# A 12-sublayer decoder on one core: router logits moved into the sublayer before, routing by packed one-hots on VectorE and ScalarE, gathers of the last combination started before all expert blocks are done

## The reference

```python
logits = x @ gate_weight.T                       # 1024 x 64
scores = softmax(logits)
topk_w, topk_idx = top_k(scores, 8)
topk_w = topk_w / sum(topk_w)
order = argsort(topk_idx.reshape(-1))            # 8192 pairs (token, expert), sorted by expert
g = ragged_dot(x_repeated[order], w_gate, sizes) # each expert: 256 -> 96
u = ragged_dot(x_repeated[order], w_up, sizes)
out = ragged_dot(silu(g) * u, w_down, sizes)     # 96 -> 256
y = sum(out_back_in_token_order * topk_w)        # 8 rows per token
x = layernorm(x + y)
```

## Time and profile before

| What | Before |
|---|---|
| Median of 3 runs | 1993.46 us (1992.19 to 1999.12) |
| The profiled execution's own time | 2002.99 us |
| Its span in the trace | 2001.2 us |
| PE, DVE, ACT, POOL busy | 76%, 60%, 41%, 29% of the span |
| Moved by DMA | 126.19 MB, 63 GB/s mean |
| HBM written | 18.74 MB |

### The profile page before, as it was taken

One profiled execution on the slowest core, in us unless ns is written; L12 is line 12 of the kernel. 1 busy time (PEld: TensorE's weight loads), 2 busy tenths in 40 slices (PEclk: granted clock), 3 DMA queues, 4 the chain that ended last, 5 costly groups with the idle time before them and its releaser, 6 DMA issues. The chain is left out here.

```text
span 2001.2 us, 26001 instructions
## 1 busy us (share of the span) xinstructions
PE 1519.1 (76%) x8419; PEld 924.1 (46%) x8419; DVE 1192.4 (60%) x2274; ACT 829.3 (41%) x1630; POOL 575.2 (29%) x585
## 2 busy tenths in 40 slices
PE   6899779985267477777899987998997945999900
PEld 4656435554143122245344444335564634888800
DVE  3537642246745799987999984543365464444343
ACT  3237421213624665634999972210463101333300
POOL 0100200212020699944000001112102426555375
PEclk9999889997689699998555558998798956999955
DMA  2100000011000000001343330000000005999932
GB/s 83 58 10 2 2 21 1 24 55 48 1 29 0 0 1 0 0 1 76 59 74 73 72 64 32 0 0 1 1 2 15 1 21 172 336 342 342 313 102 87
DMA packets 117813, 126.19 MB, mean 63 GB/s; under 512 B 75088, under 2 KB 93648, under 8 KB 116272
## 3 DMA queue, kind: packets, MB, share of 16 engines
q1 hardware_dynamic: 108512, 99.48, 16.3%
q0 software_dynamic: 9168, 25.05, 3.9%
HBM read 88.97 MB, written 18.74 MB: 54 GB/s over the span
## 5 line engine op out<-in xcount | busy, mean ns | idle before, releaser
L1639 POOL TENSOR_TENSOR l_drive<-l_area,l_xpad 128x512 f32<-128x512 f32 x128 | 158.4, 1270 | 88.6 <-ACT l_xpad L1657 88.6
L436 POOL TENSOR_TENSOR rstd<-var,minus_half 128x1 f32<-128x1 f32 x96 | 61.1, 637 | 368.2 <-DVE var L407 368.2
L1613 PE MATMUL psum<-l_drive,consts 128*128 128x512 f32 x256 | 136.2, 635 | 37.7 <-DVE l_drive L1704 37.7
L2032 ACT ACTIVATE l2x_rings<-psum,l2x_mx,l2x_q_s 128x1024 f32<-128x1024 f32 x128 | 154.3, 1205 | 8.6 <-DVE l2x_mx L2003 6.5
L1989 DVE TENSOR_REDUCE l2x_mx<-psum 128x1 f32<-128x1024 f32 x128 | 155.6, 1217 | 0.9 <-PE psum L1955 0.9
L1698 DVE TENSOR_TENSOR_SCAN l_state<-psum,l_drive 128x512 f32<-128x512 f32 x128 | 152.5, 1212 | 5.1 <-ACT psum L1670 4.5
L2510 POOL DMA_INDIRECT l3f_rows<-moe_rows,l3f_token_ids x127 | 120.6, 949 | 97.8 <-PE psum L2537 90.2
L1955 PE MATMUL psum<-l2x_kT,l2x_qT 48*128 48x512 bf16 x256 | 130.0, 612 | 14.1 <-ACT l2x_rings L2032 5.8
L355 ACT ACTIVATE XT<-psum 128x256 f32<-128x256 f32 x88 | 33.9, 385 | 242.5 <-PE psum L376 242.5
L2548 PE MATMUL psum<-l3f_xT,l3f_of_expert 128*96 128x128 f32 x1016 | 134.0, 276 | 0.0
L2595 DVE COPY l3f_xT<-psum 128x256 f32<-128x256 f32 x127 | 53.9, 424 | 133.0 <-PE psum L2537 123.4
(11 more groups left out here) (477 smaller groups left out, 3340.2 us busy)
## 6 DMA issues: line engine op xcount, KB each, us to landing
l3f_of_expert<-in_experts SPq DMA_DIRECT2D x127, 320.0 KB
moe_out<-l3f_y_out SPq DMA_DIRECT2D x127, 128.0 KB
arena<-in_pack SPq DMA_DIRECT2D x1, 3660.0 KB, 12.1
arena<-in_pack SPq DMA_DIRECT2D x1, 3277.0 KB, 10.7
arena<-in_pack SPq DMA_DIRECT2D x1, 2688.0 KB, 9.8
arena<-in_pack SPq DMA_DIRECT2D x1, 2303.0 KB, 8.7
l3f_rows<-moe_rows,l3f_token_ids POOLq DMA_INDIRECT x127
arena<-in_pack SPq DMA_DIRECT2D x1, 1538.0 KB, 6.7
```

The source lines that it names most:

```text
L1613: nc.tensor.matmul(sum_bank(c), k.identity[:, :], drive[:, (4 * i + c) % 8, :], start=n == 0, stop=n == states - 1, skip_group_check=True) ...
L1639: nc.gpsimd.tensor_tensor(drive[:, (4 * i + c) % 8, :], dx[:, c, half * HALF:(half + 1) * HALF], b_copy[:, i % 2, :], ALU.mult).then_inc(d ...
L2032: nc.scalar.activation(e[:, i % 3, :], score_banks(i).rearrange("p b t -> p (b t)"), ACT.Exp, bias=mx[:, i % 4, 1:2], scale=q_s[:, i:i + 1 ...
```

## The change

Five things, all of them in the last two sublayers but one:

- `layernorm_in` takes `follow`. For l3x_out, PE makes the router logits of tile j - 1 right behind the transposes of tile j, in columns 256 to 319 of the same bank, and ACT copies them to `k.logits`. The stage l3f_logits is gone; POOL's constants and SP's store of x stand at the head of l3f_route.
- Routing: top 8 on the logits themselves; the exponentials go to ACT and are off the chain. PE counts first (`counted`) and ranks then, so that DVE sums the blocks meanwhile. The one-hots have the 8 choices innermost, so that all three operands of L2442 and L2443 have step 1 in their last dimension; the token number plus one is put in by ACT (scale) and not by POOL; PE's operands then have a step of 8 elements (16 bytes).
- The rows' ring has 64 places for both kinds of gathers; at most 8 gathers are in flight, each waits for the one 8 before to land, and the place's old block to be transposed.
- SP counts settled stores in `blocks_stored`, five blocks behind its stores. POOL reads `used` (the number of used blocks) and waits for that count alone before the 64 gathers of the combination. DVE's additions stand behind all its blocks; normalisation of tiles 0 to 3 among the last additions, of tiles 4 to 7 behind them all.
- At the start of sublayer 7 (`l2_xattn`, n == 7) ACT issues one DMA that fills all of `moe_out` (127 x 128 KB) with zeros from one 128 x 256 tile; SP waits for it before the last sublayer.

```diff
@@ layernorm_in, PE @@
+            def follow_tile(j):
+                pe.wait_ge(turned_taken, w0 + j + 1)
+                for out, lhsT, rhs, start, stop in follow_products(j, k.bank(4 + j % 4)):
+                    last = nc.tensor.matmul(out, lhsT, rhs, start=start, stop=stop, skip_group_check=True)
+                last.then_inc(follow_done, 1)
...
                     last.then_inc(rows_turned, 1)
+                    if j >= 1 and follow is not None:
+                        follow_tile(j - 1)
+            if follow is not None:
+                follow_tile(TILES - 1)
@@ l3_ffn @@
-    x_ring, w_ring, y_ring = 8, 6, 8
+    gathers = blocks + TILES * chosen
+    rows_kept, in_flight, w_ring, y_ring, settled = 64, 8, 6, 8, 5
...
-        project(k, "l3f_logits", TILES, rows_out(router, k.XT, experts),
-                lambda g, bank, eng, on_act: copy(nc, on_act, p[:, g, :], bank[:, :experts]), on_sync=store_rows,
-                on_pool=constants)
...
-        one_hot = lambda digit, i: (digit[:, i, :].unsqueeze(2).broadcast_to([P, chosen, P]),
-                                    numbers16[:, :].unsqueeze(1).broadcast_to([P, chosen, P]))
+        one_hot = lambda digit, i: (digit[:, i, :].unsqueeze(1).broadcast_to([P, P, chosen]), numbers16[:, :, :])
...
             @block_.scalar
...
+                for i in range(TILES):
+                    act.wait_ge(by_block, i + 1)
+                    nc.scalar.activation(in_block[:, i, :, :], in_block[:, i, :, :], ACT.Copy,
+                                         scale=token1[:, i:i + 1]).then_inc(scaled_ready, 1)
...
-                        last = nc.tensor.matmul(k.bank(2)[:, :P], in_slot[:, i, n, :], in_block[:, i, n, :],
+                        last = nc.tensor.matmul(k.bank(2)[:, :P], in_slot[:, i, :, n], in_block[:, i, :, n],
@@ l3f_experts, POOL @@
+                def gather(g, source, ids):
+                    if g >= in_flight:
+                        pool.wait_ge(gathered[g % in_flight], 16 * (g // in_flight))
+                    if g >= rows_kept:
+                        pool.wait_ge(x_turned, g - rows_kept + 1)
+                    nc.gpsimd.indirect_dma_start(rows[:, g % rows_kept, :], None, source,
+                                                 bass.IndirectOffsetOnAxis(ids, 0)).then_inc(gathered[g % in_flight], 16)
...
                 for b in range(blocks):
-                    if b >= x_ring:
-                        pool.wait_ge(x_turned, b - x_ring + 1)
...
+                    gather(b, k.moe_rows, token_ids[:, b:b + 1])
+                last_used = pool.value_load(used[0:1, 0:1], min_val=T * chosen // P, max_val=blocks)
+                pool.wait_ge(blocks_stored, last_used)
+                pool.sem_inc(all_stored, 1)
+                pool.wait_ge(all_stored, 1)
+                for j in range(TILES * chosen):
+                    gather(blocks + j, k.moe_out, place_ids[:, j // chosen, j % chosen:j % chosen + 1])
+                    if j >= 40 and j % 4 == 0:
+                        rstd((j - 40) // 4)
@@ l3f_experts, SP @@
+                def stored(b):
+                    sp.wait_ge(y_stored[b % y_ring], 16 * (b // y_ring + 1))
+                    sp.sem_inc(blocks_stored, 1)
...
                     sp.dma_start(k.moe_out[b * P:(b + 1) * P, :], y_out[:, b % y_ring, :]).then_inc(y_stored[b % y_ring], 16)
+                    if b >= settled:
+                        stored(b - settled)
@@ decoder @@
+                if n == 7:
+                    @block.scalar
+                    def _(act):
+                        nc.scalar.dma_start(k.moe_out.rearrange("(b p) d -> p b d", p=P),
+                                            k.zeros[:, :].unsqueeze(1).broadcast_to([P, 63 + T * 8 // P, D])
+                                            ).then_inc(k.sem("moe_out_cleared"), 16)
```

More of the change, by code:

```diff
@@ L336, in half_of, with layernorm_in @@
     return m, slice(half * HALF, (half + 1) * HALF)
-def layernorm_in(k, label, products, extras=(), times=1.0, out_scale=None, rows=None, eps=1e-5, turned_out=None):
+def layernorm_in(k, label, products, extras=(), times=1.0, out_scale=None, rows=None, eps=1e-5, turned_out=None,
+                 follow=None):
     nc = k.nc
@@ L445, in _ @@
                 turned_out(i, k.bank(4 + i % 4)).then_inc(turned_taken, 1)
+                if i >= 1 and follow is not None:
+                    take_follow(i - 1)
+            if follow is not None:
+                take_follow(TILES - 1)
         if store is not None:
@@ L1457, in down, with logits, logits_out @@
                     for e in range(experts) for m in range(DC)]
-        layernorm_in(k, "l3x_out", down)
+        router = k.w_next("router", DC)
+        def logits(j, bank):
+            return [(bank[:, D:D + 64], k.XT[:, c, j * P:(j + 1) * P], router[:, c, :], c == 0, c == DC - 1)
+                    for c in range(DC)]
+        def logits_out(j, bank):
+            return nc.scalar.activation(k.logits[:, j, :], bank[:, D:D + 64], ACT.Copy)
+        layernorm_in(k, "l3x_out", down, follow=(k.next_loaded, logits, logits_out))
 def l2_attn(k, w):
@@ L2476, in _ @@
                 for i in range(TILES - 1):
[L2477 removed]
+                    last = nc.tensor.matmul(by_tile[:, i + 1:, :], ones_bf[:, :], kept[:, i, :].unsqueeze(1)
                                      .broadcast_to([P, TILES - 1 - i, experts]), start=False, stop=i == TILES - 2,
                                      skip_group_check=True)
[L2480 to L2482 removed]
                 last.then_inc(ranked, 1)
@@ L2528, in _ @@
                     store(b)
+                for b in range(blocks - settled, blocks):
+                    stored(b)
+                for i in range(TILES):
+                    sp.wait_ge(normed, i + 1)
+                    sp.dma_start(k.store[i], k.X[:, i, :]).then_inc(k.sem("stored"), 16)
+                sp.wait_ge(k.sem("stored"), 16 * TILES)
             @block_.tensor
@@ L2681, in _ @@
                             spread_of(i - 1)
-                        if n == 2 and i >= 3:
-                            norm(i - 3)
-                norm(TILES - 3)
+                        if n in (4, 6) and i >= 6:
+                            norm(2 * i - 12 + (n - 4) // 2)
                 spread_of(TILES - 1)
-                norm(TILES - 2)
-                norm(TILES - 1)
-            @block_.sync
-            def _(sp):
-                for i in range(TILES):
-                    sp.wait_ge(normed, i + 1)
-                    sp.dma_start(k.store[i], k.X[:, i, :]).then_inc(k.sem("stored"), 16)
-                sp.wait_ge(k.sem("stored"), 16 * TILES)
+                for i in range(TILES - 4, TILES):
+                    norm(i)
 SUBLAYERS = {0: l0_attn, 1: l0_xattn, 2: l0_ffn, 3: l1_attn, 4: l1_xattn, 5: l1_ffn, 6: l2_attn, 7: l2_xattn,
@@ L2715, in decoder @@
         k.minus_half = sb("minus_half", [P, 1])
+        k.zeros = sb("zeros", [P, D])
+        k.logits = sb("logits", [P, TILES, 64])
         k.ssq, k.inv, k.powers, k.powered = (sb(n, [P, TILES]) for n in ("ssq", "inv", "powers", "powered"))
@@ L2748, in _ @@
                 nc.vector.memset(k.ones[:, :], 1.0)
+                nc.vector.memset(k.zeros[:, :], 0.0)
                 dve.wait_ge(first, 32)
```

155 lines of the change are left out of this document (77 added, 78 removed).

## The result

The changed kernel took **2075.09 us** (median of 4 runs, 2059.29 to 2090.95), the kernel before beside it 1994.53. The ratio is 1.0375, 95% interval 1.0272 to 1.0478: **slower**, where 1936 with a range up to 1970 was forecast.

A forecast was written before the change was run, and what follows sets the result against it. Bound taken: a chain of routing, PE (or DMA) in the expert blocks, and POOL's gather issues in the combination. Routing -30, blocks and combination -29, zeros +1 make -58: from the median 1993.5 to 1936 us, range 1914 to 1970.

The forecast's parts named there:

- Part 4: Expert blocks: gathers every 1.25 us, DMA limit 350 GB/s, so 85 blocks at 1.87 us, then 1.71.
- Part 5: Combination: its 64 gathers again take 82.4 us, DVE's additions beside them; end 304 us after the first gather, -29.
- Parts 1 to 3: Logits and routing together: -30 us, the first gather moving from 1667.9 to 1638.
- Part 1: Router logits: made inside l3x_out instead of in their own stage, net -4.8 us.
- Part 2: Routing up to the one-hots: softmax off DVE's chain -3.5 us, mask to placing -0.9, one small operation -0.1.
- Part 3: Routing's one-hots: comparison 0.68 us instead of 1214 ns, PE's eight matmuls still 1.01; -20.7 us, or -12 by the upper price.
- rival 2: Routing shortens little: comparison stays 1214 ns (+8) or PE's stepped reads take up to 4 us a tile (+20); 1944 to 1956; chance 0.18.
- rival 1: Expert blocks: DMA has room, its share counts waiting packets, blocks keep 1.71 us; -72, 1921; chance 0.22.
- Part 6: Zeros for moe_out at sublayer 7: 16.65 MB in 57 us beside the weights' load, +1 us taken, bounds 0 and 70.
- rival 3: Sublayer 7: ACT's queue holds until the zeros are handed over, its first copy up to 70 us late; 2005, slower; chance 0.08.
- Rival 4: Expert blocks: PE, starved of loads, is granted 1.2 GHz part of the time; 23 us more, 1959; chance 0.07.
- Rival 5: Combination start: the register's wait is met only after the last block, 23 blocks later; +37, 1973; chance 0.03.

The follow-up runs named there:

- e10: Changed kernel, but block gather g (from the ninth on) also waits until PE has turned block g-8; combination gathers unchecked: 1983.93 us, ratio 0.9951.
- e12: Changed kernel, block gathers waiting for the turn of block g-8 and the combination's first 16 gathers for one more turned block each: 1971.61 us, ratio 0.9880.
- e15: Changed kernel, block gathers waiting for the turn of block g-4 and the combination's first 18 gathers for one more down projection each: 1969.54 us, ratio 0.9875.
- e14: Changed kernel with three chained small memsets on POOL ahead of each block gather but the first; combination gathers unchanged: 2004.39 us.
- e4: Kernel before with a ring of 32 places for block gathers, waiting only for the landing of the gather 8 back: 1990.71 us, before 1991.57.
- e18: Changed kernel without any edit, a control on a chip that showed no stall: 1938.11 us, the kernel before beside it 1991.28 (one run each).
- e3: Changed kernel with two small memsets on POOL ahead of each block gather, no wait on PE: 1933.90 us.
- e11: e3 again, the same kernel on another chip: 2059.03 us.
- e17: Changed kernel, but block gathers take a quarter of each row from other addresses, after a memset of the whole ring: 1952.12 us.

## Why the prediction was wrong, step by step

**What failed: Part 4 and Part 5, "gathers go out every 0.95 + 0.30 = 1.25 us".** They did. I priced this by the DMA engines alone, and neither a term nor a rival had it that POOL's gathers might hold up another engine. On chips B and C and in the first measurement the end comes 82 us later after the first gather (415.6 against 333.3) where -29 was forecast. That it is the pitch of the gathers is shown on such chips: the stall of the blocks goes when they are held to PE's pace (e10, e12, e15) or set 2.0 us apart (e14). The sign stood in the trace of before: DVE lost 9.1 us in five waits "for nothing in the trace's reach", all where gathers leave some 1.25 us apart, and e4's combination, the same instructions on chip A, has no such wait. The prediction names it and adds 3 us. Its first gathers, which wait for nothing either, held DVE once for 5.5 us ("remote"); the prediction has no term for that.

**Parts 1 to 3, the first gather at 1638: it was 1641.91.** Part 1: DVE starts at 1612.21 for 1617.98, -5.8 (forecast -4.8). Part 2: to the one-hots 9.82 us for 14.53, -4.7 (-4.5). Part 3: from the one-hots to the gather 19.9 for 35.4, -15.5 (-20.7). The comparison took 0.69 and 0.68 us, as taken from the earlier trace rows. The double rate in the perf-mode tier table of "VectorE: DVE Perf Modes" of the Trainium skill, and the estimate of 0.69 from it, agree with this trace. The part of rival 2 that spoke of stepped reads was half true: PE's 8 matmuls take 2.04 us at the same granted clock of 0.50, not 1.01 and not 4.0, and all eight tiles 16.0 (1624.12 to 1640.16), which set the stage's pace. Together -26 for -30.

**Part 4, blocks at 1.87 us while gathers run: false also where PE isn't held.** In e18 PE works 19.10 and 19.01 of 20 us beside them, with the DMA share at 1.03 and 368 GB/s; the last down projection starts 229.5 us after the first gather, as before (230.5), where 248 was forecast. A share near 1.00 at 340 GB/s was demand, not a limit: rival 1's mechanism.

**Part 5.** In e18 the combination begins 194.2 us after the first gather (forecast 208), its gathers take 83.1 (82.4 in the earlier trace rows), and the end comes at 289.4 (304; before 333.3): -44 for -29. By an estimate some 10 of these 44 are not the change's: 333.3 is from a chip with the hold, from an execution 9.5 us above its median, with the late signals told above. By the runs beside it on chip D, e18 gained 53.2 us; its first gather came 20.9 earlier than in the trace of before, which leaves an estimate of -32 for the rest. The forecast for the profiled execution was 1945; less 14.6 here, plus 3.9 for the first gather and 5.0 because l3x_out ended later in this run (last logits copied at 1616.25 for 1611.23), it is 1939, where 1938.11 was measured. The forecast of 1936 took another 9.5 off for the median, which e18 didn't show. That 1936 lies 2 us from it is errors that cancel, no proof of the terms.

**Part 6 and rival 3.** The zeros' DMA was issued in 0.42 us at 905.20 and landed after 58.8 (forecast 57); ACT's first instruction of sublayer 7 stood at 908.12 for 908.41. Cost: none.

**Rival 4** had a seed of it, PE starved and granted 1.2 GHz: in the held stretches the clock is 0.50 to 0.59. But PE has no more than 12 matmuls in 20 us there; the loss is in the waits. **Rival 5** is false: in e18 the register's wait ended with some 21 blocks to go (23 forecast).

## What to carry to other kernels

A wait that bounds how far an engine runs ahead may be doing a second job, keeping its issue rate down; before you take it away, look in the trace for stretches where it already isn't in force (a loop's first rounds, the last phase) and read what the other engines wait for there. An idle wait whose releaser the profile can't name is a question to settle, not 3 us to add. Count the semaphore raises that a trace holds before you read its waits: where many are missing, the profiler itself may be part of what you see. And run the control again on each chip: one kernel here (e3, e11) differs by 125 us between two chips on which the kernel before differs by 2.

## What the runs showed of the hardware

On two of the four chips, and in the first measurement, while POOL issues indirect DMAs 1.25 us apart, about one PE instruction is reported done for each; 2.0 us apart, or 1.63 in PE's own pace, PE isn't held. DVE's signals come up to 2.2 us late at that pitch. Four stores that SP issued in the held stretches took 1.39 to 1.40 us to issue, where the median is 0.43; single ones take as long on chip D (1.38), so that alone is no sign. On the two other chips no hold is seen at the same pitch. "SBUF — State Buffer" of the Trainium skill, in "Who interferes with whom", says that a DMA never contends with a compute engine. That rule is one of SBUF's ports; here those who waited for PE did wait while gathers went out, and whether by a port no run tells. What the two share isn't known. It isn't the DMA engines' time (0.36 to 0.44 busy, and POOL never waited for a landing), nor that POOL never sleeps (e14). Bytes or descriptors: e17 was to tell and met a chip without the hold, so it stays open. So does what makes the chips differ. The nearest rival is the profiler: the chips with the hold are those whose traces lack many of the semaphore raises, every run here was taken with its records, and none without, so whether the hold exists without them is open. Last, PE's matmuls with operands stepped by 16 bytes took 2.04 us per eight where packed ones took 1.01, both at a granted clock of 0.50: a factor of two.
